# A graph transformer layer pair on one core: rows of sorted edge parts made in two halves, in other slots, with more load buffers

## The reference, cut to what matters

```python
for l in range(L):                                   # L = 2
    xn = layernorm(x, ln1_g[l], ln1_b[l])
    pos = xn @ Wpos[l] + bpos[l] + deg[:, None] * Wdeg[l][0] + bdeg[l]
    xp = xn + pos
    q, k, v = (xp @ W + b for W, b in ((Wq[l], bq[l]), (Wk[l], bk[l]), (Wv[l], bv[l])))
    att = clip(einsum('ehd,ehd->eh', q[dst], k[src]) / scale, -50, 50)
    alpha = softmax of att over the edges of one dst
    aggr = segment_sum(v[src] * alpha, dst)
    x = x + (aggr @ Wo[l] + bo[l])
    x = x + gelu(layernorm(x, ln2_g[l], ln2_b[l]) @ W1[l] + b1[l]) @ W2[l] + b2[l]
out = layernorm(x0 + x)
```

## Time and profile before

| What | us |
|---|---|
| median of 3 runs | 3809.2 |
| lowest and highest run | 3791.64, 3824.87 |
| profiled execution, its time | 3805.99 |
| its span | 3804.0 |

### The profile page before, as it was taken

The page is one execution under the profiler, slowest core; times in us unless marked ns, Lnnn a source line. Parts: engine busy times, 40 slices in busy tenths (PEclk is TensorE's granted clock), DMA queues, the critical chain, the costliest instruction groups (busy, mean ns, idle before and its releaser), DMA issues.

```text
span 3804.0 us, 74324 instructions
## 1 busy us (share of the span) xinstructions
PE 3174.2 (83%) x25705; PEld 2515.7 (66%) x25705; DVE 2900.9 (76%) x6187; ACT 1820.2 (48%) x4404; POOL 2523.6 (66%) x2470
## 2 busy tenths in 40 slices
PE   4984688889898888889898688888888888888887
PEld 3763467667676676767676476667766676666665
DVE  8985688788678878877887387777877777777776
ACT  1331255445444444544555345555555555555555
POOL 1007777777666767766676477777777767777773
PEclk7685699999899999989999699899999989998997
DMA  3015455455454545545454355555555555555552
GB/s 85 22 62 150 115 159 173 151 158 152 139 153 148 161 144 155 154 142 150 148 176 133 102 164 160 178 165 166 151 178 168 167 165 168 168 168 165 163 168 79
DMA packets 427249, 558.53 MB, mean 147 GB/s; under 512 B 78473, under 2 KB 345441, under 8 KB 426677
## 3 DMA queue, kind: packets, MB, share of 16 engines
q0 software_dynamic: 117504, 321.02, 28.4%
q1 hardware_dynamic: 301862, 225.47, 19.6%
q10 hardware_dynamic: 7506, 7.20, 0.6%
HBM read 527.98 MB, written 25.44 MB: 145 GB/s over the span
## 4 chain that ended last, share of the span: by engine, by line
PE 44%; DVE 26%; issue 8%; ACT 8%; POOL 7%; DMA 5%; SPq 2%; DVEq 1%; POOLq 0%; ACTq 0%
PE psum L951 12%; POOL kv_ring L1964 6%; PE psum L1041 5%; DVE att L1682 4%; PE psum L992 4%; PE psum L1025 3%; DVE scratch L1673 3%; PE psum L1062 3%; DVE work L1377 2%; PE psum L1008 2%; DVE kv_ring L1394 2%; PE psum L1122 2%; DMA arena<-kv_table 2%; DVE arena L1724 2%; DMA q_win<-q_table 2%
## 5 line engine op out<-in xcount | busy, mean ns | idle before, releaser
L1964 POOL DMA_INDIRECT kv_ring<-kv_table,src_idx x1840 | 1888.1, 1026 | 746.5 <-issue 543.4
L1227 ACT ACTIVATE scratch<-psum 128x512 f32<-128x512 f32 (+1 forms) x1228 | 678.1, 567 | 484.1 <-PE psum L961 305.3
L1964 POOL DMA_INDIRECT arena<-kv_table,src_idx x608 | 617.2, 1015 | 241.0 <-issue 178.0
L951 PE MATMUL psum<-arena 128*128 128x256 f32 x2156 | 677.8, 437 | 72.5 <-ACT scratch L1227 42.1
L1238 ACT COPY arena<-psum 128x512 f32<-128x512 f32 x616 | 327.1, 532 | 593.7 <-PE psum L951 578.6
L992 PE MATMUL psum<-q_win,scratch 64*128 64x128 f32 x4896 | 413.1, 316 | 160.5 <-DVE scratch L1673 80.4
L951 PEld LDWEIGHTS psum<-arena 128*128 128x128 f32 x2156 | 425.7, 218 | 179.8 <-ACT scratch L1227 57.8
L1682 DVE TENSOR_REDUCE att<-scratch 128x64 f32<-128x1024 f32 (+1 forms) x460 | 535.7, 1165 | 0.1
L992 PEld LDWEIGHTS psum<-q_win,scratch 64*128 64x128 f32 x4896 | 349.2, 215 | 262.8 <-issue 165.6
L1673 DVE TENSOR_TENSOR scratch<-psum,kv_ring 128x1024 f32<-128x1024 f32 x230 | 280.4, 1219 | 154.7 <-DMA kv_ring<-kv_table,src_idx 92.2
L1008 PE MATMUL psum<-scratch 128*64 128x136 f32 x4896 | 371.5, 296 | 31.9 <-ACT work L1321 11.5
(11 more groups left out here) (252 smaller groups left out, 4839.3 us busy)
## 6 DMA issues: line engine op xcount, KB each, us to landing
arena<-kv_table SPq DMA_DIRECT2D x154, 896.0 KB
kv_ring<-kv_table,src_idx POOLq DMA_INDIRECT x1840
q_win<-q_table SPq DMA_DIRECT2D x612, 32.0 KB
work<-kv_table SPq DMA_DIRECT2D x98, 128.0 KB
q_win<-q_table SPq DMA_DIRECT2D x154, 64.0 KB
arena<-kv_table,src_idx POOLq DMA_INDIRECT x608
work<-q_table SPq DMA_DIRECT2D x98, 64.0 KB
kv_table<-work SPq DMA_DIRECT2D x49, 128.0 KB, 2.0
```

The source lines that it names most:

```text
L951: mm = e.matmul(to[:, t % 2 * 2 * D:(t % 2 + 1) * 2 * D], hot_source[:, t * P:(t + 1) * P], source_rows[:, t, :], start=True, stop=True)
L1227: e.activation(to[:, at:at + width], apart[k % FILL_BANKS][:, 0:width], ACT.Relu, bias=1.0, scale=-1.0).then_inc(apart_read, 1)
L1964: e.indirect_dma_start(kv[m % RING_KV][:, t, :], None, kv_table[l], bass.IndirectOffsetOnAxis(ap=src_idx[:, c * T + t:c * T + t + 1], axis ...
```

## The change

Five edits belong together:

1. Block v's `source` fill goes to slot 2(v-4)+1, `rows` 0 and 1 to slot 2(v-3)+1, `rows` 2 and 3 to slot 2(v-2).
2. Query rows have four buffers instead of two, and are loaded four units ahead; source rows have two buffers; the blocks' edge rows three, and are loaded six units ahead instead of four. A layer starts with four query loads, two source loads and the edge rows of blocks in the first six units.
3. The sorting of a tile starts and ends two units earlier before its first block, and the first block of layer 0 stands after chunk 18 instead of 16 (`FIRST_B`).
4. The bias of the next q, k and v is kept as three bf16 rows (high, middle and low part) and enters PSUM as a bf16 product with three rows of ones. These parts are made with those of the other biases in the first part, on one partition.
5. The arena grows by 2240 words a partition, and the DMA scratch that is reserved for POOL's descriptors is given as 8192 bytes a partition, half of the default.

Some semaphores are merged; their waits stay where they were. The core of the diff:

```diff
-FIRST_B = 17, 4
+FIRST_B = 19, 4
+QUERIES = 4
+BLOCK_AHEAD = 6
+PLANS_B = 3
...
-ARENA = 16656
+ARENA = 18896
...
-            ahead = [("source", u + 3, h) for h in range(2) if self.is_block(u + 3)]
+            ahead = [("source", u + 4, h) for h in range(2) if self.is_block(u + 4)]
             turn = [("turn", u + 2, h) for h in range(self.parts_of(u + 2))] if u + 2 < self.nu else []
             hot = [("hot", u, h) for h in range(self.parts_of(u))]
-            rows = [[("rows", u + 2, i)] if self.is_block(u + 2) else [] for i in range(4)]
-            fills[2 * u] = turn[:1] + rows[0] + turn[1:] + rows[1] + ahead
-            fills[2 * u + 1] = hot[:1] + rows[2] + hot[1:] + rows[3]
+            rows = [[("rows", u + (3 if i < 2 else 2), i)] if self.is_block(u + (3 if i < 2 else 2)) else [] for i in range(4)]
+            fills[2 * u] = turn[:1] + rows[2] + turn[1:] + rows[3]
+            fills[2 * u + 1] = hot[:1] + rows[0] + hot[1:] + rows[1] + ahead
...
-            u = max(u, 2 * at[(s - 1) * OB] - 8 if s else 0)
+            u = max(u, 2 * at[(s - 1) * OB] - 2 * BLOCK_AHEAD if s else 0)
...
-        q_win = sb("q_win", [P, 2, D])
+        q_win = sb("q_win", [P, QUERIES, D])
...
-        b_next = sb("b_next", [P, QKV])
+        b_next = sb("b_next", [3, QKV], BF16)
...
-        source_rows = part_of(TB * 2 * D).rearrange("p (t d) -> p t d", t=TB)
+        source_rows = [part_of(TB * 2 * D).rearrange("p (t d) -> p t d", t=TB) for _ in range(2)]
...
-        plan_b = part_of(TB * P).bitcast(BF16).rearrange("p (r e) -> p r e", r=2)
+        plan_b = part_of(PLANS_B * TB * P // 2).bitcast(BF16).rearrange("p (r e) -> p r e", r=PLANS_B)
...
-                        const(b_next[:, i * D:(i + 1) * D], b[l].partition_broadcast(P))
+                        const(b_second[:, i * D:(i + 1) * D], b[1:2, :])
...
+            e.dma_start(b_next[:], bias_parts[:, :, n_rows:n_bias]).then_inc(bias_in, 16)
...
-            if m >= 2:
-                e.wait_ge(apart_made, fill(block_unit(m - 2), "hot", 1) + 1)
+            if m >= PLANS_B:
+                e.wait_ge(apart_made, fill(block_unit(m - PLANS_B), "hot", 1) + 1)
...
-            if m >= 1:
-                e.wait_ge(apart_made, fill(block_unit(m - 1), "rows", 3) + 1)
-            e.dma_start(source_rows, kv_table[l][TB * o * P:TB * (o + 1) * P, :].rearrange("(t p) d -> p t d", p=P)
-                        ).then_inc(rows_of_sources, 16)
+            if m >= 2:
+                e.wait_ge(apart_made, fill(block_unit(m - 2), "rows", 3) + 1)
+            e.dma_start(source_rows[m % 2], kv_table[l][TB * o * P:TB * (o + 1) * P, :].rearrange("(t p) d -> p t d", p=P)
+                        ).then_inc(rows_of_sources[m % 2], 16)
...
-            if n >= 2:
-                e.wait_ge(spread, 2 * (n - 1))
+            if n >= QUERIES:
+                e.wait_ge(spread, 2 * (n - QUERIES + 1))
...
-                for u in range(2):
+                for u in range(QUERIES):
                     load_queries(e, l, u)
-                load_sources(e, l, 0)
+                for b in range(2):
+                    load_sources(e, l, b)
+                for u in range(BLOCK_AHEAD):
+                    if LAYERS[l].is_block(u):
+                        load_block(e, l, LAYERS[l].units[u][1])
                 for slot in range(slots_of(l)):
                     u = slot // 2
                     if slot % 2 == 0:
-                        if u + 2 < LAYERS[l].nu:
-                            load_queries(e, l, u + 2)
-                        if LAYERS[l].is_block(u + 1) and LAYERS[l].units[u + 1][1] + 1 < LAYERS[l].ub:
-                            load_sources(e, l, LAYERS[l].units[u + 1][1] + 1)
-                        if LAYERS[l].is_block(u + 4):
-                            load_block(e, l, LAYERS[l].units[u + 4][1])
-                    elif u < LAYERS[l].nu and not LAYERS[l].is_block(u) and LAYERS[l].units[u][1] + ROWS < LAYERS[l].ca:
+                        if u + QUERIES < LAYERS[l].nu:
+                            load_queries(e, l, u + QUERIES)
+                        if LAYERS[l].is_block(u + BLOCK_AHEAD):
+                            load_block(e, l, LAYERS[l].units[u + BLOCK_AHEAD][1])
+                    elif LAYERS[l].is_block(u + 2) and LAYERS[l].units[u + 2][1] + 2 < LAYERS[l].ub:
+                        load_sources(e, l, LAYERS[l].units[u + 2][1] + 2)
+                    if slot % 2 == 1 and u < LAYERS[l].nu and not LAYERS[l].is_block(u) and LAYERS[l].units[u][1] + ROWS < LAYERS[l].ca:
                         load_plan(e, l, LAYERS[l].units[u][1] + ROWS)
...
-                e.matmul(ps[:, 0:QKV], ones[0:1, :], b_next[0:1, :], start=True, stop=False)
+                e.matmul(ps[:, 0:QKV], ones_b[0:3, :], b_next[:], start=True, stop=False)
                 e.matmul(ps[:, 0:QKV], col, w_qkv[:, l + 1, :], start=False, stop=True).then_inc(done, 1)
...
-            e.tensor_tensor(b_next[:], b_next[:], psum[:, FOLD_BANKS[3], 0:QKV], ALU.add).then_inc(wz_ready, 1)
-            e.wait_ge(wz_ready, 4)
+            e.tensor_copy(wz, psum[:, FOLD_BANKS[0], 0:QKV]).then_inc(biases_made, 1)
+            e.tensor_copy(wz_next[:], psum[:, FOLD_BANKS[1], 0:QKV]).then_inc(biases_made, 1)
+            e.tensor_tensor(b_first, b_first, psum[0:1, FOLD_BANKS[2], 0:QKV], ALU.add).then_inc(biases_made, 1)
+            e.tensor_tensor(b_second, b_second, psum[0:1, FOLD_BANKS[3], 0:QKV], ALU.add).then_inc(biases_made, 1)
...
-    nc = _bacc.Bacc("TRN2", target_bir_lowering=False, num_devices=1)
+    nc = _bacc.Bacc("TRN2", target_bir_lowering=False, num_devices=1, dynamic_dma_scratch_size=8192)
```

More of the change, by code:

```diff
@@ L528, in graph_transformer @@
         plan_ones = semaphore("plan_ones")
-        q_in = [semaphore(f"q_in{i}") for i in range(2)]
+        q_in = [semaphore(f"q_in{i}") for i in range(QUERIES)]
         apart_made, apart_read, spread = semaphore("apart_made"), semaphore("apart_read"), semaphore("spread")
@@ L630, in graph_transformer @@
         adds = [*itertools.accumulate(2 if chunk else 1 for chunk in of_chunk)]
-        q_loads = [sum(2 if of_chunk[m] else 1 for m in range(n % 2, n + 1, 2)) for n in range(units)]
+        q_loads = [sum(2 if of_chunk[m] else 1 for m in range(n % QUERIES, n + 1, QUERIES)) for n in range(units)]
         def count_width(s):
@@ L1025, in spread_queries @@
                 m = e.matmul(q_edge[f % 2][:, (t - ts[0]) * P:(t - ts[0] + 1) * P], hotT[n % 2][:, t * P:(t + 1) * P],
-                             q_win[:, n % 2, :], start=True, stop=True)
+                             q_win[:, n % QUERIES, :], start=True, stop=True)
             m.then_inc(spread, 1)
@@ L1937, in pool_first @@
             e.memset(ones_b[:], 1.0).then_inc(pool_step, 1)
-            e.memset(places[:], 0.0).then_inc(places_empty, 1)
+            e.memset(places[:], 0.0).then_inc(pool_step, 1)
             e.wait_ge(pool_step, 10)
```

79 lines of the change are left out of this document (38 added, 41 removed).

## The result

| | before | after |
|---|---|---|
| median, us | 3815.83 (4 runs, 3791.64 to 3824.87) | 3699.72 (4 runs, 3694.4 to 3709.15) |
| profiled execution, us | 3805.99 (span 3804.0) | 3694.4 (span 3692.5) |

The ratio is 0.9708, with a 95% interval of 0.9656 to 0.976. The prediction was 3700, so the size is right almost to the microsecond. Its reasons were right only in part, as the experiments show. The granted clock of the profiled execution rose too, from 0.886 to 0.904.

What follows compares the result with a forecast made beforehand. PE led (89% and 86% busy) without standing at its limit, with POOL's 2448 gathers as a floor. 45 + 74 - 9 - 2 = 108 us off 3806 gave 3698, about 3700 by the median; range 3640 to 3780.

Steps and rivals of the forecast that it cites:

- The floor: POOL's 2448 gathers in sequence; only its message waits, 133.2 us (layer 0) and 48.0 (layer 1), plus 13.4 at the end, can go.
- `rows` in other slots: Layer 0: DVE gets block sums one fill earlier; half of PE's 90.3 us standing goes, 45 us, bounds 0 and 90.
- Loads further ahead: PE's 88 us of query and source-row waits in layer 1 go; 45 us counted, bounds 15 and 61; layer 0 12 us.
- the case that POOL's floor is reached: Rival, both layers: PE and DVE never hold POOL's ring, 192 us less, 3614 us; chance 0.08.
- DVE and POOL: Gathers beside denser DVE work: could stretch, but 66 us is all so far, per gather and not per time; adds nothing.
- Gathers take longer: Sign of being wrong, on POOL: gathers were to keep the same mean of 1.02 us.
- The DMA scratch: POOL's descriptor room: halving costs nothing if POOL never waits for room; 0 us taken, bounds 0 and 66.
- The bias: Layer 0 on PE: 49 bias products in bf16 save 27.6 us, 16.7 of it in the steady window where PE leads.
- First part: DVE's casts and subtractions ahead of the layers grow from 896 to 1280 columns: 1.7 us, counted as 2 us lost.
- Blocks after chunk 18: Head of layer 0: two more chunks without blocks at POOL's pace lose 9 us of PE's time, bounds 0 and 9.
- The other sign that was to show it wrong: DVE's wait for the chunks' query rows (L992's successor), 66.8 us before, passing 100 us.
- The rival in which the block's odd slot becomes narrow: Two fills ahead of the next query rows hold DVE at 154 blocks, costing 154 us: about 3852 us; chance 0.07.

Runs made afterwards that it cites:

- The pair with 7 of 8 gathers: The kernel before and the changed kernel, each with one of the 8 gathers of each chunk left out: 3764.57 us and 3520.55 us.

## Why the prediction was right, and where it wasn't

**The floor.** Its first step, that POOL's 2448 gathers are a floor of which 133 and 48 us (and 13 at the end) were to be had, was right, and it is what held the gain. The forecast took 45 of 61 us in layer 1 and 74 less 9 in layer 0. By the first and last products layer 0 lost 65.6 us (1761.6 to 1696.1) and layer 1 37.1 us (1624.3 to 1587.2), with 5.4 us at the change of layers, 1.6 ahead and 1.9 behind. That the total meets 3700 to the microsecond is luck: layer 1 brought 8 us less than forecast, and 9 us came from places that the sum didn't count.

**"`rows` in other slots", 45 us, and "Loads further ahead", 88 us.** The places and directions were right: the waits named are gone. The terms came to 88 us in layer 1 and 74 in layer 0. The pair with 7 of 8 gathers measured 160.7 us and 76.1 us. So the sum for layer 0 was about right for what the other engines can give, and that for layer 1 was too small by nearly half. The forecast took from the waits of a window what stood outright. It had no term for a DVE that is late at one place and makes PE and ACT late at the next ones, and none for the granted clock (0.93 and 1.00 in layer 1 of this pair). How the 73 us more are shared between the two no run tells. They don't show in the time, since POOL's floor stands above them.

**What of it comes through.** The prediction gave 0.08 to the case that POOL's floor is reached, at 3614 us, and held against it that layer 0 would have to get 11% faster. POOL's waits fell from 181 to 41 us, 1.8 us of them in layer 1, and the chain runs through POOL. So the mechanism of that rival came, in layer 1 wholly and in layer 0 nearly, at the time of the forecast. The two meet because the floor itself went up.

**"DVE and POOL", 0 us.** This is the step that failed. It said that the stretch of gathers goes per gather and not per time, and added nothing; it had no count of the gathers that meet a DVE instruction that holds them. Measured: 769 gathers beside the messages' product instead of 667, 37.9 us more in gathers and 17.0 us more in "issue". That is 55 us in all, two fifths of the 140.5 us that POOL's waits gave back. The "issue" part is no delay of its own: 23 gathers waited for a message instead of 80, and each of the 57 others has 0.30 us of issue now instead. So the 133 and 48 us were never wholly to be had, since a wait for a message covers those 0.30 us. The 37.9 us are a real rise of the floor, and they are no effect of the scratch. "Gathers take longer" was among the prediction's signs of being wrong, and it came: 1.04 us instead of 1.02.

**"The DMA scratch", 0 us.** Right: 0.9991 (0.9968 to 1.0014), and a mean gather of 1019 ns. How many gathers the 8192 bytes have room for no run shows.

**"The bias", 27.6 us.** 49 products took 16.5 us (338 ns each, not 403), so 30.9 us went on PE. How much of it came through no run tells.

**"First part", 2 us.** The parts of 1280 columns took 1480 and 814 ns, 0.8 us and 0.6 us more than at 896, as counted (1.4 against 1.7). POOL's memset behind this work starts 1.8 us later, as forecast (253.76 instead of 251.95). Yet the first product started at 312.6 instead of 314.2, so it didn't reach the edges.

**"Blocks after chunk 18", 9 us.** Not tried alone, and the account of POOL has no place for a loss: its floor doesn't depend on where the blocks stand. With POOL leading nearly all through, the lower bound of 0 is the likelier one.

**The other sign that was to show it wrong.** DVE's wait for the query rows of chunks was to stay under 100 us; it went from 66.8 to 103.1. The rival in which the block's odd slot becomes narrow had this sign. It didn't decide: DVE stands 307 us for gathers, and these 36 us more seem to be hidden by them, which no run tried alone.

## What to carry to other kernels

Before an order or a buffer is changed, add up each queue's own work with its gaps, POOL's issue of DMAs above all: a queue at 69% busy can be the floor, and its waits for others, less the gap that each of them covers (0.30 us here), are the most that a change elsewhere can bring. Then ask what that queue will run into once it no longer stands: here POOL met one product of DVE more often, and 38 us came back as longer gathers, 27.5 of them beside this product. To see what a change did to the other engines, take away a slice of the work that leads, in both kernels; here that showed 244 us where the whole kernel showed 111. Compare the granted clock of the pair too. And when a queue leads, count what it does per item, as one tile less of gathered rows brought 41 us at once.

## What was not expected of the hardware

On two chips the kernel before takes 38% longer (5264.16 and 5274.57 us against 3806.81 and 3808.33), with DVE's product of the scores as long as elsewhere (L1673 over 1024 columns 1220 ns there, with the smaller scratch, and 1219 ns on a usual chip). The granted clock is lower: 0.758 to 0.775 in the kernel before and with the smaller scratch, against 0.874 to 0.892 elsewhere. The waits of one such run (the kernel before, smaller scratch) have a releaser that the profile can't name:

```profile
POOL kv_ring L1964 <- DVE scratch L1697: 1166.2, 184, 22.9
ACT scratch L1227 <- remote: 1038.0, 216, 20.0
DVE scratch L1673 <- remote: 775.1, 179, 20.7
DVE arena L1724 <- remote: 750.5, 101, 23.1
```

The timeline shows PE standing inside a run of like products, without any wait of theirs that the profile shows:

```profile
3019.52 0.18 PEld L1008 LDWEIGHTS psum<-scratch 128*64 128x64 f32 x1 [1.92 <-issue]
3020.22 0.39 PE L1008 MATMUL psum<-scratch 128*64 128x136 f32 x1 [1.71 <-issue]
...
3020.93 0.38 PE L1008 MATMUL psum<-scratch 128*64 128x136 f32 x1 [0.32 <-issue]
```

PE comes late to its own instructions in this piece (1.92 us at a weight load, 1.71 us at a product), and what helps on such a chip is another thing than on a usual one: leaving out an eighth of the gathers brought 8% of the kernel before there and 1.2% elsewhere, and the changed order with two query buffers lost 6% where it wins 2.7% elsewhere. In the profiled run with the smaller scratch the mean gather is 976 ns with DVE busy 54% of the span, and 86 of the 271 gathers beside the messages' product are long. The cause was not found, and whether the low clock is part of it or follows from the standing stays open. The changed kernel itself was not timed there.
